# A stage of attention across batch entries and eight narrow experts, rewritten by tiles, with biases, residuals and sums put into PSUM

## The reference

```python
def _L1_ffn_ref(x, ...):            # T, B, C = x.shape: here T = 4 entries, B = 512 tokens
    qkv = x @ in_proj_w.T + in_proj_b
    ...                             # 16 heads of 8 channels
    scores = jnp.einsum('tbhd,sbhd->bhts', q, k) * scale
    attn = jax.nn.softmax(scores, axis=-1)
    ctx = jnp.einsum('bhts,sbhd->tbhd', attn, v).reshape(T, B, C)
    attn_out = ctx @ out_w.T + out_b
    h = _layernorm(x + attn_out, ln1_g, ln1_b)
    flat = h.reshape(-1, C)
    probs = jax.nn.softmax(flat @ router_w.T + router_b, axis=-1)
    _, top_i = jax.lax.top_k(probs, 2)
    assign = jnp.max(top_i, axis=-1)
    out = jnp.zeros_like(flat)
    for e in range(E):              # 8 experts, 128 -> 128 -> 128
        he = jax.nn.gelu(flat @ w1[e].T + b1[e], approximate=False)
        oe = he @ w2[e].T + b2[e]
        out = jnp.where((assign == e)[:, None], oe, out)
    return _layernorm(h + out.reshape(T, B, C), ln2_g, ln2_b)
# and in the caller:
x = x + jnp.tanh(g_ffn[1]) * _L1_ffn_ref(_layernorm(x), ...)
```

## Time and profile before

| | us |
|---|---|
| median of 3 runs | 1818.79 (1818.31 to 1820.6) |
| the profiled execution, its own time | 1816.94 |
| its span, first to last instruction | 1814.8 |
| busy: TensorE matmuls | 1450.4 (80%) |
| busy: VectorE | 1212.1 (67%) |
| busy: ScalarE | 769.5 (42%) |
| busy: GpSimd | 757.0 (42%) |
| mean granted clock of TensorE | 0.887 of full speed |

### The profile page before, as it was taken

One profiled execution on the slowest core, in us unless ns is written; L12 is line 12 of the kernel. 1 busy time (PEld: TensorE's weight loads), 2 busy tenths in 40 slices (PEclk: granted clock), 3 DMA queues, 4 the chain that ended last, 5 costly groups with the idle time before them and its releaser, 6 DMA issues.

```text
span 1814.8 us, 35764 instructions
## 1 busy us (share of the span) xinstructions
PE 1450.4 (80%) x13213; PEld 970.6 (53%) x13213; DVE 1212.1 (67%) x3135; ACT 769.5 (42%) x1518; POOL 757.0 (42%) x1176
## 2 busy tenths in 40 slices
PE   4999999999999959463288789968975885858997
PEld 2777777777777748251265345523443332524555
DVE  4888788777877736448937657654457456587753
ACT  3777677666766616110044245543211443301111
POOL 4789789887767925300012343100001301133330
PEclk9999999999999979756568799988997887868998
DMA  6323222121211113300000000000000000000000
GB/s 256 94 83 113 80 63 58 43 55 46 56 41 52 47 64 98 111 0 1 0 0 1 11 5 2 1 1 1 1 1 1 1 1 1 1 1 1 7 7 12
DMA packets 35457, 64.15 MB, mean 35 GB/s; under 512 B 7528, under 2 KB 25027, under 8 KB 34132
## 3 DMA queue, kind: packets, MB, share of 16 engines
q1 hardware_dynamic: 33815, 59.77, 11.1%
q0 software_dynamic: 1472, 2.12, 0.4%
HBM read 30.59 MB, written 12.66 MB: 24 GB/s over the span
## 4 chain that ended last, share of the span: by engine, by line
PE 61%; DVE 23%; ACT 5%; issue 4%; POOL 4%; DMA 2%; SPq 0%; ACTq 0%; DVEq 0%; POOLq 0%
PE banks L496 15%; PE banks L736 6%; PE banks L764 5%; PE banks L725 5%; PE banks L1958 4%; DVE xn L442 2%; PE banks L471 2%; PE banks L1944 2%; ACT work L923 2%; PE banks L1870 2%; PE banks L2650 1%; DVE norm_room L406 1%; PE banks L1911 1%; PE banks L1601 1%; PE banks L1414 1%
## 5 line engine op out<-in xcount | busy, mean ns | idle before, releaser
L1031 POOL TENSOR_TENSOR work<-work 128x512 bf16<-128x512 f32 (+1 forms) x512 | 358.7, 723 | 76.8 <-ACT work L923 75.9
L436 POOL TENSOR_TENSOR norm_room<-norm_room,minus_half 128x4 f32<-128x4 f32 x48 | 50.1, 1044 | 535.2 <-DVE norm_room L411 535.0
L808 DVE TENSOR_REDUCE work<-banks 128x1 f32<-128x666 f32 x256 | 216.3, 845 | 68.9 <-PE banks L725 67.0
L930 ACT ACTIVATE work<-banks,work 128x666 f32<-128x666 f32 x256 | 208.0, 813 | 35.7 <-DVE work L808 27.9
L923 ACT ACTIVATE work<-banks 128x512 f32<-128x512 f32 x256 | 152.8, 597 | 145.2 <-PE banks L736 144.9
L725 PE MATMUL banks<-work 128*128 128x512 bf16 (+1 forms) x1024 | 187.6, 306 | 7.7 <-DMA work<-work 7.6
L736 PE MATMUL banks<-const,work 128*128 128x128 f32 x1024 | 159.1, 278 | 14.5 <-ACT work L923 11.5
L496 PE MATMUL banks<-work,weights_b 128*128 128x512 bf16 (+1 forms) x840 | 161.1, 351 | 11.4 <-DVE work L2285 4.7
L471 PE MATMUL banks<-const,xn 128*128 128x128 f32 x176 | 39.8, 367 | 133.9 <-DVE xn L442 83.6
L477 ACT ACTIVATE xt<-banks 128x512 f32<-128x512 f32 x48 | 28.7, 597 | 271.0 <-PE banks L471 271.0
L725 PEld LDWEIGHTS banks<-work 128*128 128x128 bf16 x1024 | 95.8, 98 | 86.5 <-DMA work<-work 8.5
(11 more groups left out here) (417 smaller groups left out, 3223.3 us busy)
## 6 DMA issues: line engine op xcount, KB each, us to landing
work<-work SPq DMA_DIRECT2D x128, 166.5 KB, 3.0
sorted<-in_pads SPq DMA_DIRECT2D x10, 838.5 KB
weights_b<-in_weights SPq DMA_DIRECT2D x1, 4120.0 KB, 24.1
work<-scratch SPq DMA_DIRECT2D x64, 64.0 KB, 2.0
weights_b<-in_weights SPq DMA_DIRECT2D x1, 2824.0 KB, 9.3
weights_a<-in_weights SPq DMA_DIRECT2D x1, 2056.0 KB, 8.3
weights_a<-in_weights SPq DMA_DIRECT2D x1, 2050.0 KB, 10.1
work<-work SPq DMA_DIRECT2D x32, 64.0 KB, 1.9
```

What stands on the lines that cost most here:

```text
L808: ve.tensor_reduce(self.neg_max[i % 4], self.slot[i % 2][:, 0:KEYS0], AX_X, ALU.max, negate=True).then_inc(self.mark("max"))
L930: ac.activation(self.probs[i % 3], self.slot[i % 2][:, 0:KEYS0], ACT.Exp, bias=self.neg_max[i % 4]).then_inc(self.mark("exp"))
L1031: po.tensor_tensor(parts[:, :, :, 0], exact, parts[:, :, :, 1], ALU.subtract).then_inc(self.mark(event, i - 3))
```

## The change

Stage 3 is worked in another order and with other instructions:

- A tile j is now part j of all four entries (`place_rows`). Attention runs tile by tile on VectorE: scores of tiles 0 and 1, values of 0 and 1, scores of 2, and so on. GpSimd does one of the four query rows' products for j < 3. The weighted values of four entries are summed by TensorE in PSUM, by products with the identity (`batch_mix_pe`), which also turns them.
- Biases and residuals become matmuls into the same bank: a bf16 matrix `lead` with two rows of ones multiplies the bias, stored as a high and a low row. ScalarE evicts the projections. The first norm reads PSUM; its gain and bias are applied by ScalarE when it evicts the turned tile.
- Routing is done for eight tiles at a time. The experts run over four groups of 512 tokens: groups 0 and 1 are tiles j = 0 and 1 of all entries; groups 2 and 3 are tiles 2 and 3 of entries 0, 1 and of entries 2, 3. The experts of groups 0 and 1 begin when tiles 0 to 2 have been through attention (tile 2's norm and tile 3's work stand between expert steps of `between`).
- The choice of an expert is put in front of Gelu: a bf16 product adds -1e30 to the tokens that don't belong to it (`unless3`), so that Gelu gives zero, and the down products of all eight experts and the residual are summed in one bank (`batch_down_pe`). VectorE's accumulation goes. Up and down products are three bf16 products each; GpSimd makes each low part in place.
- The closing reads that bank; gain is multiplied by the gate in advance (`gain3`), and the bias times the gate is added to x in advance (`base3`).
- Low parts of this stage's and of stage 5's weights are made by GpSimd in place in the stage before (`batch_ahead_po`), so that stage 5 reads them with a stride of two.
- The follow norm of entry 2 moves into stage 4's list, at 0.2, 0.6 and 0.9.

The core of the diff (removed lines of the rewritten functions are those printed above):

```diff
--- before.py
+++ after.py
...
+    b["lead"] = np.zeros((P, P), np.float32)
+    b["lead"][[0, WIDE]] = 1.0
...
+        for at in (0, WIDE):
+            sp.dma_start(self.small[at:at + EXPERTS, :], d["small"]).then_inc(mark("dma_small", n=16), 16)
...
+        self.batch_ahead_po(po)
...
     def batch_pe(self, pe):
+        w = self.w[3]
         self.barrier(pe, 3)
         pe.wait_ge(*self.at("dma_weights3", 16))
+        pe.wait_ge(*self.at("dma_const_b", 16))
+        pe.wait_ge(*self.at("bias_parts3", 3))
+        for j in range(QT):
+            for b in range(BATCH):
+                if j == 0:
+                    if b == BATCH - 1:
+                        self.follow_turn(pe, 2, b)
+                    self.columns(pe, 2, b)
+                n, t = BATCH * j + b, QT * b + j
+                bank = self.bank(pe, n % 4, "qkv_kept3", n)[:, 0:3 * P]
+                pe.matmul(bank, self.cb["lead"], self.in_bias3, start=True, stop=False)
+                pe.matmul(bank, self.xt[:, t * P:(t + 1) * P], w["in"], start=False, stop=True).then_inc(self.mark("projected3", n))
+        for j in (0, 1):
+            self.batch_mix_pe(pe, j)
+            self.batch_out_pe(pe, j)
+        for j in (0, 1):
+            self.batch_turn_pe(pe, j)
+            self.batch_logits_pe(pe, j)
+        self.batch_mix_pe(pe, 2)
+        self.batch_out_pe(pe, 2)
+        for g in (0, 1):
+            self.batch_hot_pe(pe, g)
+        between = {6: (self.batch_mix_pe, 3), 7: (self.batch_out_pe, 3), 9: (self.batch_turn_pe, 2), 10: (self.batch_logits_pe, 2),
+                   11: (self.batch_turn_pe, 3), 12: (self.batch_logits_pe, 3), 15: (self.batch_hot_pe, 2), 16: (self.batch_hot_pe, 3)}
+        for k in range(BATCH * EXPERTS + 3):
+            if k in between:
+                piece, n = between[k]
+                piece(pe, n)
+            if k < BATCH * EXPERTS:
+                self.batch_up_pe(pe, k)
+            if k >= 3:
+                self.batch_down_pe(pe, k - 3)
+        for b in (0, 1):
+            self.follow_turn(pe, 3, b)
+
...
+    def batch_mix_pe(self, pe, j):
+
+        bank = self.bank(pe, 7, "columns", "mixed", j)
+        for t in range(BATCH):
+            pe.wait_ge(*self.at("weighted3", j, t))
+            for s in range(BATCH):
+                m = pe.matmul(bank[:, t * P:(t + 1) * P], self.weighted3[j % 2][:, t, s, :], self.eye, start=s == 0, stop=s == BATCH - 1)
+        m.then_inc(self.mark("turned", "mixed", j))
+
+    def batch_out_pe(self, pe, j):
+
+        bank = self.bank(pe, 5 + j % 2, "normed", "heads", j)
+        pe.wait_ge(*self.at("columns", "mixed", j))
+        for t in range(BATCH):
+            out, own = bank[:, t * P:(t + 1) * P], self.xt[:, (QT * t + j) * P:(QT * t + j + 1) * P]
+            pe.matmul(out, self.cb["lead"], self.out_bias3, start=True, stop=False)
+            pe.matmul(out, own, self.eye, start=False, stop=False)
+            m = pe.matmul(out, self.mixed3[j % 2][:, t * P:(t + 1) * P], self.w[3]["out"], start=False, stop=True)
+        m.then_inc(self.mark("brought3", j))
...
+    def batch_up_pe(self, pe, k):
+
+        g, x = k // EXPERTS, k % EXPERTS
+        if x == 0:
+            pe.wait_ge(*self.at("small_columns", 3, g))
+            pe.wait_ge(*self.at("x_low3", g))
+        if g == 0:
+            pe.wait_ge(*self.at("up_low3", x // 4))
+        if k == 0:
+            pe.wait_ge(*self.at("unless3", 1))
+        bank = self.bank(pe, 1 + k % 2, "gelu3", k)
+        chosen = self.halves(self.hot3_t[:, g * SEQ:(g + 1) * SEQ])[:, :, 1]
+        pe.matmul(bank, self.unless3[:, x, :], chosen, start=True, stop=False)
+        of = self.halves(self.w[3]["w1"][:, x * P:(x + 1) * P])
+        wide, shape = self.group_of(bank, g), self.group_columns(self.xt, g)
+        by = shape.bitcast(BF16).rearrange("p b (n s) -> p b n s", s=2)
+        m = self.products(pe, wide, lambda part: of[:, :, 1 - part], lambda part: by[:, :, :, 1 - part], False, True)
+        m.then_inc(self.mark("up3", k))
+
+    def batch_down_pe(self, pe, k):
+
+        g, x = k // EXPERTS, k % EXPERTS
+        bank = self.bank(pe, 3 + g % 2, "added3", g) if x == 0 else self.bank_of(3 + g % 2)
+        if x == 0:
+            pe.wait_ge(*self.at("bias_parts3", 3))
+            for i, t in enumerate(self.group_tiles(g)):
+                out, own = bank[:, i * P:(i + 1) * P], self.halves(self.xt[:, t * P:(t + 1) * P])
+                at = (4 * g + i) * P
+                pe.matmul(out, self.halves(self.hot3_t[:, at:at + P])[:, :, 1], self.down_bias3, start=i == 0, stop=False, skip_group_check=True)
+                for part in (1, 0):
+                    pe.matmul(out, own[:, :, part], self.cb["eye_b"], start=False, stop=False, skip_group_check=True)
+        if g == 0:
+            pe.wait_ge(*self.at("down_low3", x // 4))
+        pe.wait_ge(*self.at("hidden_low3", k))
+        of, by = self.halves(self.hidden3[k % 4]), self.halves(self.w[3]["w2"][:, x * P:(x + 1) * P])
+        for i in range(4):
+            for of_hidden, of_weights in ((1, 1), (0, 1), (1, 0)):
+                m = pe.matmul(bank[:, i * P:(i + 1) * P], of[:, i * P:(i + 1) * P, of_hidden], by[:, :, of_weights],
+                              start=False, stop=x == EXPERTS - 1, skip_group_check=True)
+        m.then_inc(self.mark("down3", k))
...
     def batch_ac(self, ac):
         w = self.w[3]
         self.barrier(ac, 3)
+        ac.wait_ge(*self.at("dma_weights3", 16))
         self.follow_turned(ac, 2, BATCH - 1)
+        for j in range(QT):
+            for b in range(BATCH):
+                n, t = BATCH * j + b, QT * b + j
+                ac.wait_ge(*self.at("projected3", n))
+                ac.activation(self.qkv3[:, t, :], self.bank_of(n % 4, 3 * P), ACT.Copy).then_inc(self.mark("qkv_kept3", n))
+            if j == QT - 2:
+                self.batch_exp_ac(ac, 0)
+        self.batch_exp_ac(ac, 1)
+        self.batch_mixed_ac(ac, 0)
+        self.batch_exp_ac(ac, 2)
+        self.batch_mixed_ac(ac, 1)
+        for j in (0, 1):
+            self.batch_heads_ac(ac, j)
+        self.batch_mixed_ac(ac, 2)
+        self.batch_router_ac(ac, 0)
+        for g in (0, 1):
+            self.batch_hot_ac(ac, g)
+        between = {3: (self.batch_exp_ac, 3), 6: (self.batch_mixed_ac, 3), 9: (self.batch_heads_ac, 2), 11: (self.batch_heads_ac, 3),
+                   14: (self.batch_router_ac, 1), 15: (self.batch_hot_ac, 2), 16: (self.batch_hot_ac, 3)}
+        for k in range(BATCH * EXPERTS):
+            if k in between:
+                piece, n = between[k]
+                piece(ac, n)
+            x = k % EXPERTS
+            if k >= 4:
+                ac.wait_ge(*self.at("down3", k - 4))
+            ac.wait_ge(*self.at("up3", k))
+            ac.activation(self.hidden3[k % 4], self.bank_of(1 + k % 2), ACT.Gelu, bias=w["b1"][:, x:x + 1]).then_inc(self.mark("gelu3", k))
+        for b in (0, 1):
+            self.follow_turned(ac, 3, b)
+
...
+        ac.activation(columns, self.bank_of(7).rearrange("p (b n) -> p b n", b=BATCH), ACT.Identity, bias=self.w[3]["ln1_b"],
+                      scale=self.w[3]["ln1_g"]).then_inc(self.mark("columns", "heads", j))
...
     def batch_ve(self, ve):
         self.barrier(ve, 3)
         self.follow_measure(ve, 2, BATCH - 1)
         self.follow_scale(ve, 2, BATCH - 1)
+        for piece, j in ((self.batch_scores_ve, 0), (self.batch_scores_ve, 1), (self.batch_values_ve, 0), (self.batch_values_ve, 1),
+                         (self.batch_scores_ve, 2), (self.batch_measure_ve, 0), (self.batch_scale_ve, 0), (self.batch_measure_ve, 1),
+                         (self.batch_scale_ve, 1), (self.batch_values_ve, 2), (self.batch_router_ve, 0),
+                         (self.batch_scores_ve, 3), (self.batch_values_ve, 3), (self.batch_measure_ve, 2), (self.batch_scale_ve, 2),
+                         (self.batch_measure_ve, 3), (self.batch_scale_ve, 3), (self.batch_router_ve, 1)):
+            piece(ve, j)
+        for g in range(BATCH):
+            self.batch_close_ve(ve, g)
+            if g == 2:
+                for b in (0, 1):
+                    self.follow_measure(ve, 3, b)
+                for b in (0, 1):
+                    self.follow_scale(ve, 3, b)
+
...
+    def batch_scores_ve(self, ve, j):
+
+        score, most, last = self.score3[j], self.most3[j], BATCH - 1
+        sums = lambda a, z: ve.tensor_reduce(score[:, a:z, :, :].rearrange("p t s h -> p (t s h)"),
+                                             self.product3[:, a:z, :, :].rearrange("p t s (h d) -> p (t s h) d", d=8), AX_X, ALU.add)
+        ve.wait_ge(*self.at("qkv_kept3", BATCH * j + last))
+        if j < last:
+            self.batch_product(ve, j, 0, last).then_inc(self.mark("multiplied3", j))
+            ve.wait_ge(*self.at("multiplied3", j))
+            sums(0, last)
+            ve.wait_ge(*self.at("product3", j))
+            i = sums(last, BATCH)
+        else:
```

(76 more changed lines are left out.)

355 lines of the change are left out of this document (143 added, 212 removed).

## The result

The changed kernel takes 1765.12 us (median of 4 runs, 1761.98 to 1765.68), the kernel before 1818.55 in the same set: ratio 0.9702, 95% interval 0.9689 to 0.9714. That is 53.4 us less, where 62.6 less were forecast; the time lies inside the range (1740 to 1785). The profiled execution took 1764.95, its span 1763.1.

The account below looks back on a forecast made before the run. VectorE was taken to bound the attention, TensorE the experts. Terms -60.1 - 3.2 - 3.8 + 1.5 + 3 = -62.6 from the profiled 1816.94 gave 1754.3, as a median 1756 us; range 1740 to 1785.

Parts of the forecast that it names:

- Attention, -60.1 forecast: Stage entry to first expert: 57.0 us in place of 117.1.
- routing ..., to 870.1: End of attention: VectorE's routing of eight tiles, 5.2 us following values 2, which end at 864.9.
- TensorE at the lower clock sets the attention: Rival, attention: TensorE's lower clock there adds 12 us, giving 1768; chance 0.12.
- Experts, -3.2 forecast: Expert loop: 63.2 us of work plus 9.5 of stops, together 72.7 in place of 75.9.
- The stops, forecast 9.5: Expert loop: pipeline fill 2, exponential 2.5, copies 1, second routing 2, lower clock at the start 2.
- 2 at step 15: Expert loop: a 2 us stop for the second routing, also holding the rest of the table switches' cost.
- 2.5 for the exponential at step 3: Expert loop: a 2.5 us stop, with table switches of 1.28 us each partly hidden by two up banks.
- GpSimd as the rival: Expert loop: GpSimd's subtraction sets the step, at 2.0 us the loop grows 13.4, giving 1770; chance 0.09.
- The overlap: Steps 6, 7, 9, 15: tile 3's 23 us of VectorE lie beside expert steps; failing rival 1774, chance 0.12.
- Closing, -3.8 forecast: Last down product to next stage's first matmul: 4.3 us in place of 8.1.
- The stage before, +1.5 forecast: Preceding stage: GpSimd's added preparation slows VectorE beside it, +1.5 us, bounds 0 and 4.
- Behind, +3 forecast: Next stage: entry 2's follow norm put before entry 3's delays it, +3 us, bounds 1 and 5.

Follow-up runs that it names:

- e3: Changed kernel plus 26, 14 and 12 unread 384-column products keeping TensorE busy in the attention; median 1766.67 us, ratio 0.9709.
- e4: Changed kernel without GpSimd's 32 subtractions for the hidden values' low halves, the down product reading the high halves again; median 1760.59 us, ratio 0.9682.
- e7: Changed kernel with one of the down product's three products (low half of the weights) left out; median 1753.33 us, ratio 0.9645.
- e5: Changed kernel with tile 3's and the second routing's exponentials replaced by copies, removing the loop's four table loads; median 1762.14 us, ratio 0.9698.
- e2: Changed kernel with the second routing's exponential at step 12 instead of 14, both one-hot turns at step 16; median 1762.46 us, ratio 0.9691.
- e6: Changed kernel with GpSimd's two clearings moved behind tile 1's work and follow powers to steps 30 and 31; median 1757.89 us, ratio 0.9670.
- e8: Changed kernel with GpSimd's preparation in the stage before begun only after the last entry's follow turn; median 1758.64 us, ratio 0.9661.

## Why the prediction was right, and where it was off

The measured gain is 9 us short of the forecast one. The misses of the attention, the experts and what lies behind have one sign, the experts' being the largest, and the upper bounds had room for them.

**Attention, -60.1 forecast, -58.7 measured.** The prices were right: scores 5.1 to 5.6 (5.4), values 4.07 (4.15), two norms 8.4 (7.6), routing 5.4 without its stand (5.2). The step that failed is "routing ..., to 870.1": it put the exponential at once behind VectorE, although ScalarE's queue had a copy ahead of it that waits for TensorE. The routing took 10.2 us. It cost only 2.9 because the term beside it, TensorE's 8.5 us for tile 2's sums and output product "partly at the lower clock", was itself near the end: it took 5.95 + 0.9 + 2.2 = 9.0. The rival "TensorE at the lower clock sets the attention" was true in its place, behind the queue's order, and not in its size: e3 shows tile 2's sums at 3.8 with the clock kept, 2.1 less, and the attention 1.4 shorter, not 12.

**Experts, -3.2 forecast, +1.8 measured: the largest miss.** The work term is mis-sized by 1.9 (32 steps of 1.64 for 1.58; what the step holds is TensorE alone, by e4 and e7). The openings, tile 3's products, turns and logits take 12.4 us of the rows for 12.6. The stops, forecast 9.5, are then about 12.8 (77.7 less 32 x 1.64 and less 12.4). "2 at step 15" took 5.42, and the lower clock behind it 2.1 more (924.04 to 928.65, 4.6 us for work of 2.5); "2 of lower clock at the start" took 2.3 (4.97 for three steps of 0.90). "2.5 for the exponential at step 3" is a stand of TensorE of 0.65, and all four table loads cost about 1.8 (e5); "2 to fill the pipeline" and "1 for copies" show no stand. What was left out: that the exponential of step 14 stands behind two Gelus (e2: 4.6 us with its order changed), and that GpSimd's queue stops the last two subtractions behind the follow powers (a stand of 1.24; e6: 1.0).

**GpSimd as the rival.** It does not set the step (1.04 to 1.14 each, the step unmoved in e4), but it doubles VectorE's times beside it, 2.50 to 5.03 us for four products of tile 3. The forecast priced that for the stage before only. With the hole at the end it is 3 to 4 of the 5.1 us by which e4's loop is shorter; the rest lies ahead of GpSimd's first subtraction.

**The overlap** holds at steps 6, 7 and 9, where TensorE does not wait for VectorE, and fails at 15: a part of that rival, 5 of its 18 us.

**Closing, -3.8 forecast, -4.1 measured**: right, term by term (0.89 + 0.38 + 0.17, power 1.01, updates 1.14).

**The stage before, +1.5 forecast.** In the nine profiles of kernels that leave it alone it takes 60.4 to 67.0, median 64.4; before the change 61.8 and 63.4. That is +1.8, within the bounds, but less than the spread of the nine; the first profile alone would have said +5.2. "The neighbour stretches VectorE" was right: the scale takes 2.02 to 2.87 us in all nine, 1.11 in the three with e8's edit and 1.11 and 1.26 before. What was missing is that TensorE's 16 products behind it then take up to 5.04 us (2.96 in the three).

**Behind, +3 forecast, +5.0 between the two pairs of profiles.** Entry 3's power in the next stage answers to the earlier trace rows:

```profile
964.46 0.24 POOL L2280 TENSOR_SCALAR work<-weights_c 128x1 f32<-128x1 f32 x1 [1.33 <-DVE x L1891]
...
994.72 1.02 POOL L444 TENSOR_TENSOR norm_room<-norm_room,minus_half 128x4 f32<-128x4 f32 x1 [8.48 <-DVE norm_room L419]
```

It comes 30.3 us behind GpSimd's first instruction of the stage, 27.6 before: +2.7, as forecast. It lasts: VectorE's first instruction of `masked_ve` comes 62.3 to 63.9 us behind that cut in all twelve profiles of changed kernels, and 59.8 in both of before.

But +5.0 for all that lies behind is a sum with luck in it. Up to TensorE's first instruction of the last stage (`mixture_pe`) the two profiles of the changed kernel take 599.8 and 596.3 us, those of before 587.8 and 587.9: +8.4 and +12, where +3 were forecast. The last stage itself takes 198.9 us in six of the twelve, 205.3 to 207.1 in the other six, and 207.2 in both of before. Neither the change nor an experiment's edit touches it. What differs is TensorE's granted clock: in the 75 us that end 50 us before the kernel's end it is 1.00 in those six and 0.91 or 0.93 in the other eight profiles. The windows of the changed kernel, first and second profile (the clock is the third number from the end):

```profile
1638.10:1713.10 75.00, 67.56 (x406) 37.63 (x405) 56.85 (x118) 14.98 (x42) 29.94 (x29) 1.00 0.03 8
```

```profile
1637.90:1712.90 75.00, 68.21 (x374) 37.82 (x376) 50.84 (x108) 14.38 (x41) 28.11 (x27) 0.91 0.03 8
```

So "behind" falls into two groups, 794.3 to 795.3 in four profiles and 798.6 to 802.5 in eight (in two of the eight, the changed kernel's first and e2, the last stage was short and the one before it 3.5 us longer). Whether the kernel before can reach the short value no profile shows, so part of the median's gain may be the clock's.

Of the +8 to +12 one more part is located: 331 us into it 48 products of the later feed-forward stage take 4.50 to 5.26 us in all twelve, 2.84 in both of before, after the same stand of 3.56 us and at a granted clock of 0.50 in the changed kernel. The stride of the weights does not do it: 48 such products at full clock just ahead take 2.93, and 2.84 before. Why the clock falls there now, and what picks between the two values of the last stage, stays open.

## What to carry to other kernels

When a wait is forecast for an engine, read the queue of the one that ends it: what stands ahead of that instruction, and on whom does that wait? Three losses found here (5.07, 4.17 and 1.24 us of standing) were of this kind, and moving a line or two brought them to 0.32, 0.32 and 0.74. And cut the span at events before comparing medians: here 7 us came and went in stages that no edit touched, more than any single edit was worth. Even inside a stage, ask whether the gain lies where the edit acts: of the 2.9 us by which e5 and e6 each shortened the loop, 1.1 lay ahead of anything that they changed.

## What the runs showed of the hardware

GpSimd beside VectorE stretches some of its instructions and not others. Element-wise ones that read SBUF grow: products of 512 from 0.63 to 1.26 each, 64 elements from 0.22 to 0.69 and 0.96, a scale from 1.11 to 2.73 for four. Sums along an axis (L1807, 2048 elements: 2.34 in two parts beside GpSimd, 2.29 in one without it; L521 and L524 0.22) and what reads PSUM (L450 from PSUM 1.37, L1885 1.12) do not. GpSimd is slowed too, three subtractions in 4.11 for 3 x 1.04. The Trainium skill ("GPSIMD Engine Reference", section "Key points") names shared SBUF interfaces, for instructions of VectorE with two SBUF inputs or in a two-port mode; the trace agrees for those with two SBUF inputs (the products of 512), and whether the scale, which has one, ran in such a mode no run here shows.

In the stage before, TensorE's clock was at the lower level behind a stand of 3.49 us (16 products in 5.03) and at full behind one of 1.87 (2.96); stands of 2.02 and 2.85 were followed by 4.13 and 4.15 us, between the two, and one of 2.87 in e4 by 2.96. So the length of the stand alone does not tell the clock behind it. The kernel before had the slower products too, in its second profile (behind 2.02): part of what looked like a loss from the change is chance.
